# Gated cross-attention and a routed feed-forward layer on one core: one query pair turned through DRAM, and the joint between the two stages ordered anew

## What is computed

```python
x = x + tanh(g_xattn) * xattn(layernorm(x), ctx, ctx, ...)   # stage one, then its residual
x = x + tanh(g_ffn) * ffn(layernorm(x), A, B, Wr)            # stage two

# xattn, per element; the 128 tokens are the channels c, the 1024 features are the positions n
qh, kh, vh = (Wq @ q, Wk @ k, Wv @ v)       # each 8 heads x 64 rows x 1024 positions
qh = softmax(qh over the 64 rows of a head) * 64**-0.5
kh = softmax(kh over the 1024 positions)
out = Wo @ (per head: (vh @ kh.T) @ qh) + bo
return out / norm_over_c(out) * g * sqrt(128)

# ffn: the 16 best of 64 rank-16 experts per token
gates = softmax(top16(x @ Wr.T)); h = (x @ A) * gates; return (h @ B) * 2
```

## Time and profile before

| | |
|---|---|
| median of 3 runs | 942.69 us (940.84 to 943.14) |
| the profiled execution | 941.5 us, of which the span of its records is 939.5 us |
| busy PE / DVE / ACT / POOL | 902.3 / 740.4 / 687.1 / 515.6 us |
| granted TensorE clock, mean | 0.989 |
| stage one | up to about 561 us, some 32.4 us an element |
| stage two | the rest, 23 us an element |

### The profile page before, as it was taken

How to read it: one execution, slowest core, us unless ns; L and a number is a source line. 1 busy time by engine, 2 the same in 40 slices (tenths; PEclk the granted TensorE clock), 3 DMA queues, 4 the chain that set the end, 5 groups by cost and what they waited for, 6 DMA issues and landing times.

```text
span 939.5 us, 15942 instructions
## 1 busy us (share of the span) xinstructions
PE 902.3 (96%) x4732; PEld 765.1 (81%) x4732; DVE 740.4 (79%) x1517; ACT 687.1 (73%) x1408; POOL 515.6 (55%) x340
## 2 busy tenths in 40 slices
PE   7899999999999999999989998599999999999997
PEld 5687888887787888788878787599999999999886
DVE  6888889988898898889877768687777777777631
ACT  4787797778768777876776747678888888888732
POOL 3786678788878978887787944222222222222100
PEclk9999999999999999999999999799999999999999
DMA  4324433453544335333412883111121111111001
GB/s 156 115 88 139 156 113 119 152 181 104 166 159 145 115 131 174 100 124 112 160 50 83 270 304 119 57 68 68 68 68 68 68 68 67 67 67 67 23 23 46
DMA packets 35175, 104.04 MB, mean 111 GB/s; under 512 B 4416, under 2 KB 11584, under 8 KB 35136
## 3 DMA queue, kind: packets, MB, share of 16 engines
q1 hardware_dynamic: 29376, 82.59, 25.3%
q0 software_dynamic: 5472, 20.45, 6.9%
q10 hardware_dynamic: 288, 0.52, 0.2%
HBM read 79.43 MB, written 24.12 MB: 110 GB/s over the span
## 4 chain that ended last, share of the span: by engine, by line
PE 66%; POOL 9%; DVE 8%; issue 8%; ACT 7%; DMA 1%; POOLq 0%; ACTq 0%; SPq 0%; DVEq 0%
PE ps L61 20%; PE ps L63 19%; PE ps L62 19%; PE ps L1437 4%; PE ps L1446 3%; POOL qe L447 3%; ACT qe L679 2%; POOL ctx_lo L406 2%; ACT h_raw L772 1%; PE ps L1427 1%; POOL qhalf L440 1%; ACT qT_hi L687 1%; POOL aT_lo L460 1%; POOL xn_lo L426 1%; ACT y_raw L772 1%
## 5 line engine op out<-in xcount | busy, mean ns | idle before, releaser
L518 POOL TENSOR_TENSOR rb<-u_in,rb 128x1024 f32<-128x1024 f32 x14 | 33.7, 2405 | 233.8 <-DVE rb L990 233.8
L447 POOL TENSOR_TENSOR qe<-qe,qrec 128x1024 f32<-128x1024 f32 x64 | 121.2, 1903 | 15.0 <-DVE qrec L1008 15.0
L61 PE MATMUL ps<-aT_hi,yT_hi 128*128 128x448 f32 (+2 forms) x360 | 119.8, 333 | 0.9 <-DVE yT_lo L1143 0.9
L772 ACT ACTIVATE h_raw<-hg 32x256 f32<-32x256 f32 x256 | 106.3, 415 | 17.7 <-DVE hg L1157 14.9
L62 PE MATMUL ps<-aT_hi,yT_lo 128*128 128x448 f32 (+2 forms) x360 | 118.6, 329 | 0.0
L63 PE MATMUL ps<-aT_lo,yT_hi 128*128 128x448 f32 (+2 forms) x360 | 118.4, 329 | 0.0
L440 POOL TENSOR_TENSOR qhalf<-qe 128x512 f32<-128x512 f32 x64 | 82.2, 1284 | 63.5 <-ACT qe L679 61.6
L1014 DVE TENSOR_TENSOR qT_lo<-ps,qT_hi 128x512 fp32r<-128x512 f32 x128 | 81.5, 678 | 34.8 <-ACT qT_hi L687 34.3
L61 PE MATMUL ps<-bT_hi,hT_hi 128*128 128x512 f32 x240 | 94.5, 394 | 2.7 <-DVE bT_lo L1049 2.3
L772 ACT ACTIVATE y_raw<-u_in 32x256 f32<-32x256 f32 x224 | 92.8, 414 | 3.3 <-DVE u_in L1148 0.8
L62 PE MATMUL ps<-bT_hi,hT_lo 128*128 128x512 f32 x240 | 94.2, 393 | 0.0
(11 more groups left out here) (178 smaller groups left out, 2559.6 us busy)
## 6 DMA issues: line engine op xcount, KB each, us to landing
x_in<-in_x SPq DMA_DIRECT2D x16, 512.0 KB, 3.3
ctx_in<-in_ctx SPq DMA_DIRECT2D x16, 512.0 KB, 5.5
ctxT_in<-in_ctxT SPq DMA_DIRECT2D x16, 512.0 KB, 3.3
ctxT_hi<-in_ctxT POOLq DMA_DIRECT2D x16, 512.0 KB, 4.1
u_scratch<-osb SPq DMA_DIRECT2D x16, 512.0 KB, 3.0
out<-res SPq DMA_DIRECT2D x16, 512.0 KB, 2.8
x<-in_x SPq DMA_DIRECT2D x15, 512.0 KB, 3.9
turn_scratch<-ek SPq DMA_DIRECT2D x14, 512.0 KB, 4.4
```

What stands on the lines that cost most here:

```text
L61: nc.tensor.matmul(psum, whi, mhi, start=start, stop=False)
L447: nc.gpsimd.tensor_tensor(v, v, w, ALU.mult).then_inc(q_norm, 1)
L772: last = nc.scalar.activation(dst[32 * q:32 * q + 32, 256 * a:256 * a + 256], src[32 * a:32 * a + 32, 256 * q:256 * q + 256], ACT.Copy)
```

## The change

- **Query pair 0 through DRAM.** `exp_q(b,0)` writes its tile in a permuted order; `halve` and `normalise` of pair 0 follow that order (the second as two instructions). DVE's new `turn_q` transposes 32x32 blocks after `max_q(b,2)`; SP's new `move_q` writes 512 KB to DRAM and reads them back in four transfers. `hi_q(b,0)` and `lo_q(b,0)` now read the moved tile in SBUF, in the next body ahead of `hi_kc` and `lo_kc`. `tr_q(b,0)` is gone from PE.
- **Order inside elements.** ACT: `hi_q(b-1,1)` before `exp_k(b,1)`, `hi_moved_k` after `exp_q(b,1)`. DVE: `sum_q(b-1,3)` after `max_k(b,1)`, `lo_q(b-1,1)` before `scale_m`, `max_q(b,1)` before `max_k(b,2)`, the second half of `std` after both. POOL: `halve(b,0)` between the two `normalise`, `lo_a` at the start of the next body, `lo_moved_k` after `normalise(b,0)` and the DMA of `hi_c`. PE: `shift_q(b,1)` before `output(b-1,0)`.
- **The joint.** `early_newton` after `halve(14,2)`. In body 16 `y` goes before the queries. POOL takes strips 2 to 7 of B, DVE only 0 and 1 and earlier. In the first two bodies of stage two `sum_u` comes after `up(b,1)`, and `result(0)`, `part_u(4)`, `lo_moved_h(1)` come before `stats2(3)`. A has one semaphore a strip.
- **The end.** Of the last `h`, ACT moves half and DVE the other half; the last output is stored in two halves.

```diff
 def exp_q(b, p):   # ACT
-    if started(b):
-        act.wait_ge(q_T, 8 * b + 2 * p - 6)
+    if started(b) and p == 0:
+        act.wait_ge(q_lo, 8 * b - 6)
+    elif started(b):
+        act.wait_ge(q_T, 6 * b - 6 + 2 * p)
...
+        if p == 0:
+            to = qe[:, 0, :].rearrange("p (q n i) -> p n q i", q=P // 32, i=32)
+            of = psQ.rearrange("p a (n q i) -> p (a n) q i", q=P // 32, i=32)
 def hi_q(b, p):    # ACT
+    if p == 0:
+        act.wait_ge(q_moved, MOVED * (b + 1))
+        for h in range(2):
+            nc.scalar.activation(turned_q(qT[0], h), moved_q(h), ACT.Copy).then_inc(q_hi, 1)
+        return
 def lo_q(b, p):    # DVE
     for h in range(2):
         dve.wait_ge(q_hi, 8 * b + 2 * p + h + 1)
+        if p == 0:
+            nc.vector.tensor_tensor(turned_q(qT[1], h), moved_q(h), turned_q(qT[0], h).bitcast(f32),
+                                    ALU.subtract).then_inc(q_lo, 1)
+            continue
+def turn_q(b):     # DVE
+    dve.wait_ge(q_norm, 4 * b + 1)
+    nc.vector.transpose(qe[:, 0, :], qe[:, 0, :]).then_inc(q_turned, 1)
+def move_q(b):     # SP
+    wait_apart(sp, sp_turns, (q_turned, b + 1))
+    sp.dma_start(turn_q_dram, qe[:, 0, :]).then_inc(q_put, 16)
+    wait_apart(sp, sp_turns, (q_put, PUT * (b + 1)))
+    for q in range(P // 32):
+        sp.dma_start(qe[32 * q:32 * q + 32, 0, :].rearrange("j (a f) -> j a f", f=256),
+                     turn_q_dram.rearrange("(a j) (q f) -> q j a f", a=P // 32, f=256)[q]).then_inc(q_moved, 16)
 def body(...)      # SP: between the load of x and the load of ctxT
+    if head:
+        move_q(b)
 def body(...)      # POOL
     if tail:
-        normalise(b - 1, 2)
-        normalise(b - 1, 3)
+        normalise(b - 1, 2)
     if head:
         halve(b, 0)
+    if tail:
+        normalise(b - 1, 3)
...
-    if head and turned(b):
-        lo_moved_k(b)
     if head:
         normalise(b, 0)
         hi_c(b)
+        if turned(b):
+            lo_moved_k(b)
...
 def body(...)      # DVE, from its start on, for an element in the middle
     sum_q(b-1,2)  turn_k(b)  stats(b+1)  std(b+1, 0..2)
-    sum_q(b-1,3)  lo_kc(b-1)  max_q(b,0)  max_k(b,1)  std(b+1, 3..)
-    scale_m(b-1)  lo_q(b-1,1)  max_k(b,2)  max_q(b,1)  sum_q(b,0)
+    lo_q(b-1,0)   lo_kc(b-1)  max_q(b,0)  max_k(b,1)  sum_q(b-1,3)
+    lo_q(b-1,1)  scale_m(b-1)  max_q(b,1)  max_k(b,2)  std(b+1, 3..)  sum_q(b,0)
     lo_q(b-1,2)  max_k(b,3)  max_q(b,2)
+    turn_q(b)
     lo_k(b,1)  lo_q(b-1,3)  max_k(b+1,0)  sum_q(b,1)  lo_k(b,2)  max_q(b,3)  lo_k(b,3)
-    lo_q(b,0)
 def body(...)      # PE
     output(b - 1, 1, range(CH // 2, CH))
-    tr_q(b, 0, next(turn))
 def by_pool(k):
-    return k in (2, 3, 5, 7)
+    return k >= 2
 def ffn_body(i, j) # PE
     up(b, 0)
-    if norms:
+    if norms and not late:      # late: b is 1 or 2
         sum_u(b + 2)
     up(b, 1)
+    if norms and late:
+        sum_u(b + 2)
 def ffn_body(i, j) # DVE, first body (b = 1)
     lo_moved_h(0)
-    lo_b(1)
-    for n in range(3):
-        route_step(1, n)
     turn_y(2, 0)
-    lo_b(4)
...
-    lo_b(6)
...
-    norm_u(b + 2)
+    norm_u(3)
+    result(0, 0, 0, 0)
+    part_u(4)
+    lo_moved_h(1)
     stats2(3, ...)
+def move_last_h(): # DVE, groups 2 and 3; ACT's move_h(15) keeps 0 and 1
+    dve.wait_ge(h_turned, NB)
+    ...
+    nc.vector.tensor_copy(h_raw[32 * q:32 * q + 32, 256 * a:256 * a + 256],
+                          hg[32 * a:32 * a + 32, 256 * q:256 * q + 256])
```

More of the change, by code:

```diff
@@ L521, in residual, with body @@
                 nc.gpsimd.tensor_tensor(x2b[slot][:, :], rb[:, :], x2b[slot][:, :], ALU.add).then_inc(x2_done, 1)
-            def body(b, head, tail, ahead, split=False):
-                if split:
+            def body(b, head, tail, ahead, low=False, cast=False):
+                if low:
+                    lo_a(b - SPLIT - 1)
+                if cast:
                     cast_a(b - SPLIT)
@@ L571, in body @@
                     halve(b, 2)
+                if isinstance(b, int) and b == NB - 2:
+                    early_newton()
                 if head and not ahead:
@@ L585, in _ @@
             pool.sem_inc(a_low, 1)
[L586 to L589, removed]
+            body(SPLIT, head=True, tail=True, ahead=True, cast=True)
+            with pool.Fori(SPLIT + 1, SPLIT + DC) as b:
+                body(b, head=True, tail=True, ahead=True, low=True, cast=True)
+            body(SPLIT + DC, head=True, tail=True, ahead=True, low=True)
             body(NB - 2, head=True, tail=True, ahead=True)
@@ L783, in move_h @@
                 act.wait_ge(h_turned, b + 1)
-                move_groups(h_raw, hg, h_moved)
+                move_groups(h_raw, hg, h_moved, range(2 if isinstance(b, int) and b == NB - 1 else P // 32))
             def hi_moved_y(b):
@@ L844, in body @@
                     exp_q(b, 1)
+                if head and turned(b):
+                    hi_moved_k(b)
                 if tail and head and not turned(b):
@@ L1223, in body @@
                     std(b + 1, range(3))
-                if tail and head:
-                    sum_q(b - 1, 3)
                 if tail:
+                    lo_q(b - 1, 0)
                     lo_kc(b - 1)
-                if tail and not head:
-                    sum_q(b - 1, 3)
                 if head and started(b):
@@ L1319, in _ @@
             lo_y(1)
+            stats2_sums(2, 2)
             gated(0, 2)
             turn_h(0)
+            lo_b(0)
+            lo_b(1)
             part_u(EARLY)
-            stats2(2, 2)
-            lo_b(0)
+            std2(2, range(NCH + 1))
+            for n in range(3):
+                route_step(1, n)
             def ffn_body(i, j):
@@ L1530, in up @@
                 for m in range(DC):
+                    if p == 0 and not started(b):
+                        pe.wait_ge(a_ready[m], 16)
                     last = three_pass(psH[p], rows_T(b)[0][:, m, :], rows_T(b)[1][:, m, :], aT[0][:, m, v], aT[1][:, m, v],
@@ L1599, in body @@
                         tr_k(b, 0, next(turn))
+                if head and turned(b):
+                    shift_q(b, 1)
                 if tail and head:
                     output(b - 1, 0, range(CH // 2))
-                if head:
+                if head and not turned(b):
                     shift_q(b, 1)
```

146 lines of the change are left out of this document (85 added, 61 removed).

## The result

The changed kernel takes 996.98 us (median of 4 runs, 995.54 to 997.17) against 941.77 for the kernel before (940.37 to 943.14): 1.058 times as long, 95% interval 1.056 to 1.060. The forecast was 954.9 with a range from 922 to 978. The profiled execution has a span of 993.9 us, 54.4 more than before, and a mean granted clock of 0.981.

The account below looks back on a forecast made before the run. PE, 96% busy but held in a loop through DVE's lo_k(b,3). Thirteen periods +24, element 14 -2.2, element 15 0, joint -7.7, end -1.6: +12.2 unrounded on 941.5, 953.7; median 1.2 higher: 954.9 us, range 922 to 978.

Parts of the forecast that it names:

- Part 1: End of element on PE: dropping tr_q(b,0), 1.15 us, gains only 0.65, since the next context (C') waits for lo_k(b,3).
- Part 2: Middle of element, from max_q(b,0)'s start (M): new DVE and POOL order starts tr_k(b,2) 1.1 us later, at M+19.6.
- Part 3: lo_q(b-1,0) ahead of max_q(b,0), DVE held by POOL: M 1.4 us later, C+8.5 (C: context's start); bounds 0 and 2.6.
- The rival of the clock: PE's waits halve its clock for 3 us an element, adding 1.5 us each: 975 us, slower; chance 0.12.
- Part 4: Way through DRAM: moved tile there by C'+1.5, hi_q asks at C'+4; costs nothing, covered by 2.5 us.
- Element 15, taken at nothing: Last element loses tr_q(15,0), gains Part 3's wait and spread_first ahead of mts: 0 us, bounds -1.5 and +3.
- Parts 5 and 6: Joint: PE's waits shrink, -7.7 us, bounds -14 and -4. End: earlier last copies and half-size last store, -1.6 us.
- element 14: Its period of 36.54 us, with early_newton ahead of lo_ctx, falls to 34.3: -2.2 us.
- Slower: Sign of the whole change: time above the kernel before, beyond about 3 us; chance 0.57.
- part 5: Joint: 10.63 us wait for part_u(4) goes, sum_u(5) waits instead; 8 us gained, taken -7.7, bounds -14 and -4.

Follow-up runs that it names:

- third kernel: Changed kernel with query pair 0 back over TensorE (no turn_q, no move_q), new order inside elements and new joint kept: 951.1 us, ratio 1.011.
- fourth kernel: Kernel before with only the new joint, new place of early_newton and new end; elements in old order and over TensorE: 932.5 us, ratio 0.990.
- run 12: Changed kernel with POOL's cast_a DMA issue moved from ahead of halve to ahead of mts in elements 5 to 12: 969.5 us, ratio 1.030.
- Run 6: Fourth kernel plus the first query pair through DRAM, its steps placed where DVE and POOL are free, without tr_q(b,0): 952.5 us, ratio 1.012.
- first kernel: Changed kernel with lo_q(b,0) reading PSUM in place of the moved tile, leaving one SBUF input: 952.1 us, ratio 1.012.
- run 13: Changed kernel with lo_a back mid-body and, in elements 5 to 12, POOL's wait for exp_q(b-1,3) ahead of cast_a's issue: 1008.9 us, ratio 1.072.
- runs 9 and 10: Changed kernel with useless bn_stats on DVE ahead of lo_q(b-1,0), one instruction in the former, two in the latter: 1004.0 and 1015.0 us.
- run 10: Changed kernel with two useless bn_stats instructions (1.24 us in all) on DVE straight ahead of lo_q(b-1,0): 1015.0 us, ratio 1.078.

## Why the prediction was right in kind and wrong in size

- **Part 1 (the loop gives back 0.65, not 1.15): right.** From `tr_k(b,2)` to C' it is 6.38 us (6.35 forecast), and in elements 2 to 12 it is 6.4 to 6.6 in every kernel with the way through DRAM, against 6.98 without. Against TensorE's way in the same order, DRAM without the port saves 0.4 an element (33.8 to 33.4); in the old order nothing (32.5 against 32.65), since the middle of the element grows by as much.
- **Part 2 (+1.1 by the order): the mechanism was right, the size too small.** The two `normalise` instructions take 2.1, and POOL's chain has the order reckoned. But `tr_k(b,2)` starts at M+19.8 (M+19.6 forecast), which is 1.4 later than before in elements with `lo_a` (5 to 12), of which the prediction read one, and 2.0 later in the others, where it had been at M+17.8. The third kernel's periods are 1.3 over the fourth's.
- **Part 3 (M = C+8.5): the term that failed.** In elements 1 to 4 it is C+8.41 to C+8.48, by the mechanism named; the tenth is luck, since DVE came at C+5.3 instead of C+5.0. There M had been at C+7.5 to C+7.8 before in elements 2 to 4, not C+7.12, so that 0.7 to 1.0 and not 1.4 was added: the errors of this term and of part 2 partly cancel in the period of 34.7. In 5 and 13 it is C+7.8. In elements 6 to 12 it is C+10.5 to C+10.6, outside the upper bound of C+9.7, since that bound let DVE in between two of POOL's instructions, where it was held for the whole row of three. The rows that it rested on, held only the kind that takes turns. The diff had the cause in sight, `cast_a` straight ahead of `halve` with `lo_a` in front of it to use up the wait between; the prediction didn't cost these two at all. In all, 997.0 - 969.5 (run 12): 27.5 us of the 42 that the forecast missed.
- **The rival of the clock** was priced about right (1.5 an element; 1.6 in the mean of elements 7 to 12, none in 6) and stood as a case of its own, with 0.12. It came with the longer wait: in the changed kernel's elements PE waits up to 1.7 and the clock stays, it waits 3.34 to 3.40 and it falls. But the length of the wait alone doesn't decide: element 6 waits 3.42 and keeps its clock. A second step hung on the upper bound of part 3.
- **Part 4 (DRAM at nothing): right up to element 14.** The write took 3.2 us, the reads 2.8, and no wait of the changed kernel names the moved tile. Run 6 shows how near the end of the cover was: asked for 3 us sooner, beside the strips of A, it was 8 us late. **Element 15, taken at nothing, costs 6.5,** over its bound of 3: DVE, with no statistics of x to take, comes early and waits 4.07 us for `hi_q(14,0)`, which on ACT stands behind `exp_q(14,3)` (3.39) and, there alone, the scaling of `u_first` (1.27), and PE waits 2.06 for `mts`, which POOL forms behind `spread_first(0)`. The first kernel, free of the port, has the same 40.0 there.
- **Parts 5 and 6, and element 14:** together -11.5 forecast. The fourth kernel has -8.7: element 14 gains more (-4.85 for -2.2), the joint and the end 7.7 for 9.3, and element 15 loses 3.6. The changed kernel itself gained only 3.1 of the 9.3 for joint and end: among other things the last pair, in body 16, takes 3.66 us beside POOL, and PE waits 2.79 for the `lo_kc` behind it, a wait that the fourth kernel doesn't have. So of the 14.6 us that run 12, without the dear kind, still lies over the forecast, some 8 are in element 15, 6 behind it and 1 in element 14. The wait of 10.63 has gone, and those that take its place are in the list of the fourth kernel's waits (engine, tile and line, releaser; us in total, times, longest):

```profile
PE ps L1543 <- DVE part L1212: 4.6, 1, 4.6
PE ps L61 <- DVE yT_lo L1176: 3.7, 1, 3.7
```

  The first is `sum_u(5)`, forecast at about 6.
- **The sign and the range.** Slower was given 0.57, on the grounds of parts 2 and 3, and it is slower. The range of the forecast itself, 944 to 968, is narrower than its own bounds: M at either bound in 14 elements and part 5 at either bound make some 929 to 975. Even 975 leaves out the result, because the dear kind, the clock that fell with it and element 15 lie outside these bounds.

## What to carry to other kernels

Work taken off the busiest engine is worth only what the loop around it gives back: 96% busy said nothing of the 1.15 us, the end of `lo_k(b,3)` 0.8 us ahead of C' said nearly all. When a step is moved, ask of each of DVE's operations with two inputs in SBUF what POOL does beside it, and whether a DMA issue of POOL stands straight ahead of that row: the issue elsewhere, or ahead of a wait, was worth 27 us here. And look at every kind of element before costing one: the dear ones were the seven with two more calls of POOL's in them, and the one element that was read before costing was not like the first four.

## What the runs showed of the hardware

- A DVE instruction with two inputs in SBUF and POOL's instructions hold each other up, in turns or not. Two subtractions of 128x512, 0.68 us each with one input in SBUF, take 2.4 to 3.9 us beside a row of POOL's that had no DMA issue straight ahead of it, and no half waits there for more than one of POOL's instructions. They take 4.1 to 5.8 when a DMA issue of POOL's stood straight ahead of the row, and then they are held to its end. The Trainium skill ("SBUF — State Buffer", SBUF: two separate sides) says that whichever starts first gets the shared ports for the whole instruction; the first kind agrees, the second is longer than that: three of them. What inside the issue does it isn't shown.
- Coming later doesn't help: in the dear kind, asked for 0.3, 0.9 and 1.5 us into the row and in run 13 ahead of it, the pair ended 1.2 us after the row's end. In the cheap kind it costs: 3.2 to 3.9 us instead of 2.6 when DVE came after the end of the row's first instruction (runs 9 and 10).
- In stage one of the changed kernel PE's granted clock fell to 0.50, for some three to seven us, after six waits of 3.34 to 3.40 us, and not after one of 3.42; after waits of up to 2.8 it stayed full. The length of the wait alone doesn't tell: in run 10 it also fell after waits of 2.5 and 1.9.
